# Expert rows scattered to choice and token order instead of gathered; five score banks in the last attention turn of each pass

## The reference, cut to what is computed

```python
def ffn(hs):                       # hs: (8, 512, 256), 16 heads of 8 channels
    Q, K, V = heads(hs @ q_w), heads(hs @ k_w), heads(hs @ v_w)
    ao = softmax(Q @ K.T / sqrt(8)) @ V             # (8, 512, 128)
    mla = concat([ao, 0]) @ o_w
    probs = softmax(mla @ router_w)                 # 8 experts
    topw, topi = top_k(probs, 2); topw /= topw.sum()
    expert = gelu(mla @ w1[e]) @ w2[e]              # for each expert e
    return hs + 0.3 * sum(topw * expert[topi])

x = x + 0.5 * ffn(layernorm(x))
x = x + segment_attention(layernorm(x))   # 8 heads of 64, segments of 64, running memory
x = x + 0.5 * ffn(layernorm(x))           # the same weights
```

## Time and profile before

| what | us |
|---|---|
| median of three runs (2219.89 to 2227.61) | 2226.52 |
| the profiled execution, its own time | 2226.73 |
| its span, first to last instruction | 2225.0 |
| busy in the span: PE, DVE, ACT, POOL | 1844.2, 1480.0, 932.0, 553.3 |
| expert stages: first to last start of a y | 643.7 to 834.1 and 1940.5 to 2131.0 |
| gathers of the mixer: first to last start | 840.8 to 1144.1 |
| gathers of the combine: first to last start | 2134.7 to 2215.5 |

### The profile page before, as it was taken

How to read it: one execution, slowest core, us unless ns; L and a number is a source line. 1 busy time by engine, 2 the same in 40 slices (tenths; PEclk the granted TensorE clock), 3 DMA queues, 4 the chain that set the end, 5 groups by cost and what they waited for, 6 DMA issues and landing times. The chain is left out here.

```text
span 2225.0 us, 40905 instructions
## 1 busy us (share of the span) xinstructions
PE 1844.2 (83%) x12392; PEld 1023.6 (46%) x12393; DVE 1480.0 (67%) x3529; ACT 932.0 (42%) x1694; POOL 553.3 (25%) x640
## 2 busy tenths in 40 slices
PE   1899999999759994999999963899999998499930
PEld 1443333332259982677766641233333332299920
DVE  2578898888244444888888653888888883354433
ACT  0146666666512222444444410266666667122200
POOL 2221233331122214211110001223333311322256
PEclk9789999999979996999999975799999999699965
DMA  8326333321022223111110015344333220122245
GB/s 197 62 50 136 70 57 70 72 57 21 11 76 71 71 70 128 32 39 39 39 39 11 11 41 107 63 91 118 66 64 69 59 31 13 59 74 71 71 141 184
DMA packets 154622, 153.21 MB, mean 69 GB/s; under 512 B 20364, under 2 KB 145036, under 8 KB 154124
## 3 DMA queue, kind: packets, MB, share of 16 engines
q1 hardware_dynamic: 113600, 98.95, 19.7%
q10 hardware_dynamic: 30636, 27.21, 4.5%
q0 software_dynamic: 10240, 25.18, 4.0%
HBM read 86.60 MB, written 58.20 MB: 65 GB/s over the span
## 5 line engine op out<-in xcount | busy, mean ns | idle before, releaser
L590 DVE TENSOR_REDUCE f_M<-bank 128x1 f32<-128x512 f32 x1024 | 672.6, 685 | 179.9 <-PE bank L868 170.1
L498 ACT ACTIVATE f_PT<-bank 128x512 f32<-128x512 f32 x1024 | 571.0, 595 | 282.8 <-PE bank L885 277.9
L868 PE MATMUL bank<-f_KS,f_QS 96*128 96x512 bf16 x1024 | 404.2, 401 | 59.4 <-DVE f_M L590 27.1
L885 PE MATMUL bank<-f_QS,f_KS 99*128 99x512 bf16 x1024 | 392.5, 387 | 45.1 <-ACT f_PT L498 31.4
L885 PEld LDWEIGHTS bank<-f_QS,f_KS 99*128 99x128 bf16 x1024 | 99.6, 99 | 422.5 <-ACT f_PT L498 316.8
L895 PE MATMUL bank<-f_PT,f_V 128*32 128x512 f32 x2048 | 271.3, 603 | 0.0
L868 PEld LDWEIGHTS bank<-f_KS,f_QS 96*128 96x128 bf16 x1024 | 101.5, 100 | 179.6 <-DVE f_M L590 110.6
L1129 PE MATMUL bank<-f_room,f2m_gT 128*128 x568 | 136.2, 383 | 0.2 <-issue 0.2
L1129 PE MATMUL bank<-f_room,f1m_gT 128*128 x568 | 135.9, 383 | 0.1
L427 POOL DMA_INDIRECT routed_rows<-f_AO,f_rows_i x128 | 124.5, 973 | 42.0 <-issue 42.0
L1065 ACT ACTIVATE f2m_gT<-f2m_hb 128x512 f32<-128x512 f32 x71 | 44.7, 630 | 154.9 <-DVE f2m_hb L1086 154.9
(11 more groups left out here) (254 smaller groups left out, 2929.7 us busy)
## 6 DMA issues: line engine op xcount, KB each, us to landing
f_QS<-q_parts SPq DMA_DIRECT2D x192, 64.0 KB
f_KS<-k_parts SPq DMA_DIRECT2D x168, 64.0 KB
expert_rows<-f1m_y ACTq DMA_DIRECT2D x71, 128.0 KB, 1.8
expert_rows<-f2m_y ACTq DMA_DIRECT2D x71, 128.0 KB, 1.7
xr<-f_xr SPq DMA_DIRECT2D x16, 512.0 KB, 3.1
f_room<-in_L_ffn_w SPq DMA_DIRECT2D x2, 4096.0 KB, 21.9
q_parts<-f_q SPq DMA_DIRECT2D x16, 384.0 KB, 2.5
k_parts<-f_k SPq DMA_DIRECT2D x16, 384.0 KB, 2.5
```

The costliest lines, as they stand in the source:

```text
L498: act.activation(PT[:, i % 8, :], SCE[i % 2][:, :], ACT.Exp).then_inc(probs_ready, 1)
L590: dve.tensor_reduce(M[:, t, h:h + 1], SCM[(a * SC + i) % 3][:, :], AX.X, ALU.max).then_inc(scm_drained, 1)
L868: pe.matmul(SCM[(a * SC + i) % 3][:, :], QS[par][0:K_MAX, h, t * P:(t + 1) * P], KS[par][0:K_MAX, h, :], start=True, stop=True).then_inc(s ...
L885: pe.matmul(SCE[i % 2][:, :], KS[par][0:K_EXP, h, t * P:(t + 1) * P], QS[par][0:K_EXP, h, :], start=True, stop=True).then_inc(sce_filled, 1)
```

## The change

Routed rows get two more columns (`TAIL`): the row that the token's first choice has in `xs`, and the token's number. An expert tile finds from them where each of its rows belongs: choice 0 if the row's own place (`OWN`) is the one written in it, else choice 1; DVE computes `dest`, one row number per partition, in three operations per tile, each waiting for the one before. POOL then scatters y by `dest`, so `ys` is in order of choice and token. The rows that fill up an expert's last tile carry a choice of -1 and a spare row of their own for each expert; tiles past the end go to rows set aside (`KEEP`, `ASIDE`). Each scatter has a carrier column of its own and waits for no other scatter. The mixer and the combine load rows with plain DMAs; the combine has buffers for all batches, its residual rows are loaded during the second expert stage, and its stores go out on ACT's queue. The loop of expert slots is written out. In the last attention turn of a pass the scores of batch e use the banks `SCE + SCM`. `make_tables` loses the five operations for `IDX` and gains those for the new tables.

```diff
+TAIL = 2
@@ attend_and_route
+        WIDE = SCE + SCM
+        def score_bank(a, i):
+            return WIDE[i % len(WIDE)] if a == END - 1 else SCE[i % 2]
+        def score_bank_free(a, i):
+            if a < END - 1:
+                return a * SC + i - 1
+            if i < len(SCE):
+                return a * SC
+            return a * SC + i + 1 - len(WIDE) if i >= len(WIDE) else 0
...
-                eng.dma_start(xs[ds(at, P), :], zero_rows[:, :]).then_inc(pads_stored, 16)
+                eng.dma_start(xs[ds(at, P), :], zero_rows[:, e, :]).then_inc(pads_stored, 16)
...
-            pool.memset(zero_rows[:, :], 0.0).then_inc(init, 1)
...
-                            act.activation(PT[:, i % 8, :], SCE[i % 2][:, :], ACT.Exp).then_inc(probs_ready, 1)
+                            act.activation(PT[:, i % 8, :], score_bank(e, i)[:, :], ACT.Exp).then_inc(probs_ready, 1)
...
-                s.own(dve.tensor_scalar(ROW[:, ds((a - START) * T, T), :], rows_f[:, :, :], 0.0, None, ALU.add))
+                dve.tensor_copy(AO[par][:, :, LAT], rows_f[:, :, 0])
+                dve.tensor_scalar(AO[par][:, :, LAT + 1], w["token"][:, :], float((a - START) * S), None, ALU.add)
                 dve.tensor_copy(rows_i[:, :, :], rows_f[:, :, :]).then_inc(rows_ready, 1)
...
+            dve.memset(zero_rows[:, :, 0:LAT], 0.0)
+            dve.memset(zero_rows[:, :, LAT:LAT + 1], -1.0)
+            dve.tensor_tensor(zero_rows[:, :, LAT + 1], w["rung"][:, 0:E],
+                              w["spare_row"][:, 0:1].to_broadcast([P, E]), ALU.add)
...
-                wait(pe, probs_ready, a * SC + i - 1)
-                pe.matmul(SCE[i % 2][:, :], KS[par][0:K_EXP, h, t * P:(t + 1) * P], QS[par][0:K_EXP, h, :],
+                if a == END - 1 and i == len(SCE):
+                    pe.wait_ge(scm_drained, END * SC)
+                wait(pe, probs_ready, score_bank_free(a, i))
+                pe.matmul(score_bank(a, i)[:, :], KS[par][0:K_EXP, h, t * P:(t + 1) * P], QS[par][0:K_EXP, h, :],
@@ experts, SP
-                wait(sp, xT_filled, j + (BASE - 1))
+                    wait(sp, dest_ready, BASE + j - 1)
                 sp.dma_start(XN[:, buf, :], xs[ds(at, P), :]).then_inc(x_loaded[buf], 16)
+                load_late(sp, s)
@@ experts, POOL
+            for s in SLOTS:
+                if tile(s, 0):
+                    j, buf = tile(s, 0)
+                    e = pool.value_load(tables[0:1, 0, j:j + 1], min_val=0, max_val=E - 1)
+                    wait(pool, h_filled, BASE + j - 1)
                     pool.tensor_copy(W1[:, buf, :], w["w1"][:, ds(e * F, F)]).then_inc(w1_ready, 1)
+                if tile(s, 2):
+                    j, buf = tile(s, 2)
+                    pool.wait_ge(y_ready, BASE + j + 1)
+                    pool.tensor_tensor(pool_carrier[:, j:j + 1], zero[:, :], zero[:, :], ALU.add)
+                    pool.indirect_dma_start(
+                        out=ys, out_offset=bass.IndirectOffsetOnAxis(ap=dest[:, j:j + 1], axis=0),
+                        in_=Y[:, buf, :], in_offset=None).then_inc(y_stored[buf], 16)
@@ experts, ACT
-                    act.wait_ge(y_ready, j + (BASE + 1))
-                    act.dma_start(ys[ds(j * P, P), :], Y[:, buf, :]).then_inc(y_stored[buf], 16)
@@ experts, DVE, after the copy of the turned tile
+                    dve.tensor_scalar(offset[:, j:j + 1], XN[:, buf, LAT:LAT + 1], OWN[:, j:j + 1], float(B * S),
+                                      ALU.not_equal, ALU.mult).then_inc(offset_ready, 1)
+                    dve.wait_ge(offset_ready, BASE + j + 1)
+                    dve.tensor_tensor(target[:, j:j + 1], offset[:, j:j + 1], XN[:, buf, LAT + 1:RW], ALU.add) \
+                       .then_inc(target_ready, 1)
+                    dve.wait_ge(target_ready, BASE + j + 1)
+                    dve.scalar_tensor_tensor(dest[:, j:j + 1], target[:, j:j + 1], KEEP[:, j:j + 1], ASIDE[:, j:j + 1],
+                                             ALU.mult, ALU.add).then_inc(dest_ready, 1)
@@ combine (its gathers, index copies and two-buffer loop go)
+        @block.sync
+            for b in range(B):
+                for n in range(2):
+                    at = n * B * S + b * S
+                    sp.dma_start(R[b][:, :, n, :], ys[at:at + S, :].rearrange("(t p) d -> p t d", p=P)).then_inc(rows_loaded[b], 16)
+        @block.scalar
+                act.wait_ge(y_ready, b + 1)
+                act.dma_start(x_out[b].rearrange("(t p) d -> p t d", p=P), XR[b][:, :, :]).then_inc(y_stored, 16)
@@ attention_pass (its gathers, index copies and carrier go)
+        def load_rows(eng, a):
+            for n in range(2):
+                at = n * B * S + a * S
+                eng.dma_start(R[:, :, n, :], ys[at:at + S, :].rearrange("(t p) d -> p t d", p=P)) \
+                   .then_inc(rows_loaded if a else first_loaded, 16)
             load_x(0)
+            load_rows(sp, 0)
             load(sp, la_loaded)
...
+            for a in range(1, B):
+                pool.wait_ge(rows_read, a)
+                load_rows(pool, a)
@@ macaron
-        xs = nc.dram_tensor("routed_rows", (E * REG, LAT), F32, kind="Internal").ap()
-        ys = nc.dram_tensor("expert_rows", (NT * P, D), F32, kind="Internal").ap()
+        xs = nc.dram_tensor("routed_rows", (E * REG, LAT + TAIL), F32, kind="Internal").ap()
+        ys = nc.dram_tensor("expert_rows", (2 * TOKENS + (E + 2) * P, D), F32, kind="Internal").ap()
...
+                def load_late(sp, slot):
+                    if slot == 1:
+                        load_b2(sp)
+                    if last and slot >= 8 and slot % 4 == 0 and slot // 4 - 2 < B:
+                        b = slot // 4 - 2
+                        sp.dma_start(XR[b][:, :, :], xr[b].rearrange("(t p) d -> p t d", p=P)).then_inc(xr_loaded, 16)
```

## The result

The changed kernel takes 2155.93 us (median of 4 runs, 2147.24 to 2161.11), the kernel before 2226.78 beside it: a ratio of 0.9685, interval 0.9656 to 0.9714. It is faster by 70.9 us, where 31.7 were forecast. The profiled execution took 2161.11 (span 2159.4), the longest of the four, so its stages add up to somewhat less.

| Stage | forecast, us | measured, us |
|---|---|---|
| two last attention turns (with the rest of those stages) | -19.4 | -12.8 and -12.2 |
| expert slots, first y to last y | +35.5 | +6.6 and +7.4 |
| ends of the two expert stages (and their first slots) | +10 | +4.7 and +4.4 |
| mixer | -11 | -12.1 |
| combine | -46.8 | -51.7 |

A forecast was written before the change was run, and what follows sets the result against it. It took PE to bound expert slots, ScalarE the last attention turns, and gathers the mixer's start and the combine. Terms -46.8 - 11 - 19.4 + 35.5 + 10 = -31.7 took 2226.52 to 2195 us, eight in ten 2150 to 2240.

The forecast's parts named there:

- The loop through GpSimd: Expert slots: y, scatter, W1 copy and PE's products form a two-slot loop of 5.96 us where PE needs 5.46.
- the term of +35.5 us: Expert slots: PE waits 0.50 us in every two slots, 0.25 a slot over 142 slots, +35.5 us.
- VectorE was costed at nothing: Expert slots: three chained operations, 0.66 us, make VectorE's slot 2.5 us, under the new 2.98, so 0.
- Rival (3): Expert slots: VectorE becomes the bound if new operations wait out a W1 copy; 2212 to 2297 us, chance 0.08.
- the term of -19.4: Last attention turns: five banks let ScalarE work without gaps, 46.0 to 36.3 us, 9.7 saved twice, -19.4.
- the term of -46.8: Combine: plain loads replace gathers, DMA at 330 GB/s sets it, 44.7 us instead of 91.5, -46.8.
- the bound: Combine: the fast limit of its estimate, 41 us at 367 GB/s, -50.
- Mixer's start: Start of the mixer: rows arrive at 843.6 instead of 855.37, but weights come some 4 us later; -11 us.
- The ends: End of each expert stage: the last scatter and GpSimd's drain add 5 us per stage, +10 in all.
- (1): Expert slots: the scatter hides if GpSimd's wake and issue are 0.5 us shorter, PE stays at 2.73; 2159, chance 0.13.
- (2): Expert slots: the register load queues behind the scatter, adding 0.65 to 0.97 us to the loop; 2241 to 2264, chance 0.15.
- (4): GpSimd steps count start to start (scatter 1.25, not 0.96), or combine loads run at 217 GB/s; 2213 to 2216, chance 0.12.

The follow-up runs named there:

- Run 9: Changed kernel with a second, long satisfied wait (target rows ready) ahead of the wait for y on the scatter's carrier: 2180.88 us, ratio 0.9807.
- run 2: Changed kernel with a second, long satisfied wait (target rows ready) written after the wait for y on the scatter's carrier: 2156.89 us.
- run 1: Changed kernel with GpSimd copying W1 of tile s+1 in slot s, ahead of the scatter of tile s-2: 2153.51 us, ratio 0.9671.
- run 4: Changed kernel without the scatter: ScalarE stores each tile's y to rows in a line, output not the reference's: 2149.36 us.
- run 5: Changed kernel with VectorE's three target-row operations moved behind hb and the load of the number for y, and a third x buffer: 2151.27 us.
- run 6: Changed kernel with W1 copied ahead of the scatter and VectorE's three target-row operations behind hb, with a third x buffer: 2143.52 us, ratio 0.9627.
- Run 7: Kernel before with only the five banks of scores in the last attention turns: 2203.02 us against 2225.37, ratio 0.9898.
- run 10: Changed kernel whose combine loads only the first choice's rows and adds them twice, output not the reference's: 2151.95 us, one execution.

## Why the prediction was right and wrong

**The loop through GpSimd was right, one piece of it was not.** The order y, scatter, W1 copy, PE binds as forecast. The failed step is the term of +35.5 us: "from the carrier to the scatter 0.67 ... I take 0.71 for the gap, since other cold starts show up to 0.77". It measured 0.34, and the wake 0.09 instead of 0.14: with 1.00 for the scatter, 0.62 for the copy and y's start at 0.31 the loop is 5.59 instead of 5.96, and the excess in two slots 0.13 instead of 0.50. That is 9 us in place of 35.5; the other 5 of the 14.0 measured are the longer slots of the written-out code, for which the prediction had no term. The row the gap was read from the earlier trace rows follows a wait that GpSimd's queue itself had to pass; here the wait for y rides on the carrier, the queue goes on and has the scatter read in when y comes. Run 9 put the wait back into the queue and got 0.64 and 5.94. The Trainium skill draws the same two cases ("Perfetto Trace Analysis", sections Sequencer-only Instruction and GPSIMD Engine Instruction): a sequencer-only instruction waits in the sequencer, an engine instruction is decoded first and waits in a queue of its own. Runs 2 and 9 agree: 0.34 and 0.64.

The kernel before held both cases already. In its mixer one gap is 0.77, the upper end that the prediction quotes, where the queue passed a wait just ahead of the carrier; in the seven other batches the wait for the indices rode on the carrier for 8 to 43 us, and the first gather started 0.33 after it. The second batch:

```profile
859.11 0.19 POOL L1380 TENSOR_TENSOR la_pool_carrier<-la_zero 128x1 f32<-128x1 f32 x1 [8.45 <-DVE la_idx L1466]
859.45 0.97 POOL L1383 DMA_INDIRECT la_rows<-expert_rows,la_idx  x1
```

With 0.33 from these rows the prediction's own sum gives 5.58.

**VectorE was costed at nothing, by the wrong measure.** The prediction held its three operations against a slot ("2.5, under the new 2.98, so 0"). VectorE is not full in any slot; but the operations stand between y and hb, and y, hb, Gelu and the second product are a loop of two slots too, 5.53 us. At the forecast 5.96 it would have hidden; at the real 5.59 it holds the kernel as soon as the other is gone (runs 1, 4, 5, 6). Rival (3) had the engine right, but not its reason: in the changed kernel no operation waits out a W1 copy.

**Last turns: the mechanism was right, the term of -19.4 too small.** The gaps went, as forecast. But 35.92 us of ScalarE "busy" held more than its work: a group of four took 2.16 us, while in a run a further exponential costs 0.49, so four cost 1.96. Half of the 0.2 between is the third of each four, which before started 0.58 after the second; the other half is the end of the last one, under which no next one ran. Both were paid in nearly all of the 16 groups. Run 7 measured 22.4 for both turns, the two profiles 25.0 with what else is in those stages.

**Combine: the term of -46.8 was 4.9 short**, by its rate: 330 GB/s taken, 374 measured, above the 367 of the bound (341 at a share of 0.93, taken to a full one; the share measured was 1.09). Additions close behind (run 10) did not show. **Mixer's start** came near the forecast (-11; PE started 11.6 earlier, the stage lost 12.1), but the weights did not hold PE: the gate, forecast 16 us after the first load, was in use after 13.2, and PE waited for the additions and what follows on them. **The ends** (+5 each; 5.0 and 5.4 from y's end to the next stage) came for the reason given, the drain, and in size partly by luck: the drain ended 5.9 after the last scatter's end and not 5.0, and the shorter gap and wake gave back 0.4.

**Rivals.** (1) was near in time and wrong as a mechanism: wake and gap were shorter by 0.42 of the 0.5 that it needed, so the loop does bind, only by little. (2) is false: the register load of line 1063 runs before the scatter starts, the copy 0.01 behind it. (4) is false for the same reason: start to start the scatter counts 1.01, not 1.25; and the combine's loads did not run at 217 GB/s. Not tried: the wait alone taken away, since y must be there before it is scattered.

## What to carry to other kernels

Work out every loop that goes from an engine back to itself over several tiles, not each engine's share of a slot: two loops of nearly one length hide each other, the view of waits names only the longer, and edits to one are worth little until both are made. Where an instruction must follow a wait closely, let the wait ride on a cheap instruction ahead of it, so that the queue can read in the next. Where that instruction has two waits, the order counts: in runs 2 and 9 the one written first rode on it and the queue passed the other. And work that others wait for (hb, a copy of weights) goes ahead of work that has a slot to spare (target rows, a scatter).

## What the hardware showed that was not expected

A product of two SBUF columns on VectorE took 0.16 us beside a scatter, but waited out a W1 copy in run 6:

```profile
719.03 0.62 POOL L1066 COPY f1m_w1t<-folded_w 128x512 f32 x1
719.15 0.53 DVE L1110 TENSOR_TENSOR f1m_target<-f1m_offset,f1m_xn 128x1 f32<-128x1 f32 x1
```

That is the pair for which the prediction had no row. The Trainium skill's rule ("SBUF — State Buffer", Who interferes with whom: a VectorE instruction with two SBUF inputs contends with a GpSimd one that reads SBUF) holds here, 0.53 instead of 0.16. In run 6 it costs nothing: y still starts 0.31 after the turning, as before (0.32), and the slots are PE's.

In the first stage of run 1 a slot of the written-out code is 2.97 to 3.10 us long instead of 2.80 about once in every 15; in the second stage such slots come more often, up to 3.17. Around one of them VectorE's load of a register began 0.38 us after hb did instead of 0.03, with nothing that it waited for. The spacing says more. Counting all records of VectorE and its queue, the changed kernel's first stage has five such stops, of 0.35 to 0.38 us, at 640.6, 683.1, 725.7, 768.6 and 811.1 us, and they lie exactly 256 records apart, at 17 records a slot. Run 1 has the same five, and in the second stages they lie 128 or 256 apart. So they go with the place in the written-out code and not with a wait; the loop of the kernel before shows none of them in its first expert stage. What the queue does there was not tried. In run 6 VectorE has such stops too, but also slack, and PE shows no longer slot.
